# Who reads the quads' bank, and when: reordering VectorE's queue in a four-layer attention kernel

## The reference, cut to what matters

```python
q = nx @ Wq (+ bq);  k = kv @ Wk (+ bk);  v = kv @ Wv (+ bv)     # nx: layer norm of x, scaled and shifted
a = softmax(q @ k.T / sqrt(8) (masked), axis=-1)                  # per head
x = x + (gate *) ((a @ v) @ Wo (+ bo))
```

## Time and profile before

| | us |
|---|---|
| median of 3 runs | 1131.72 (1129.71 to 1132.47) |
| the profiled execution | 1134.09 |
| its span, first to last instruction | 1131.5 |
| stages (span): `l0` | 60 to 224 |
| `l0c` | 224 to 355 |
| perceptron and layer 1 | 355 to 655 |
| `l2`, `l3s`, `l3c` | 655 to 790, to 933, to 1063 |

### The profile page before, as it was taken

One profiled execution on the slowest core, in us unless ns is written; L12 is line 12 of the kernel. 1 busy time (PEld: TensorE's weight loads), 2 busy tenths in 40 slices (PEclk: granted clock), 3 DMA queues, 4 the chain that ended last, 5 costly groups with the idle time before them and its releaser, 6 DMA issues.

```text
span 1131.5 us, 28818 instructions
## 1 busy us (share of the span) xinstructions
PE 1045.1 (92%) x11743; PEld 651.6 (58%) x11743; DVE 803.4 (71%) x1971; ACT 572.0 (51%) x801; POOL 673.9 (60%) x776
## 2 busy tenths in 40 slices
PE   6899999999988999999999699998999999998998
PEld 4445555565555775666666445555555566555476
DVE  6788888788873534676677878878888777787321
ACT  1034434566566455444444156665555656665553
POOL 6578887777864341121114588887877656587430
PEclk8699999999999999999999699999999999999799
DMA  4300000000000102000000000000000000000001
GB/s 176 132 8 3 20 12 12 21 19 13 20 21 20 39 28 88 7 6 6 6 6 18 7 13 2 2 2 2 2 1 2 2 2 2 2 2 2 1 28 47
DMA packets 9283, 22.76 MB, mean 20 GB/s; under 512 B 1393, under 2 KB 1649, under 8 KB 8769
## 3 DMA queue, kind: packets, MB, share of 16 engines
q1 hardware_dynamic: 9152, 20.94, 5.5%
HBM read 18.77 MB, written 2.15 MB: 18 GB/s over the span
## 4 chain that ended last, share of the span: by engine, by line
PE 69%; DVE 17%; issue 5%; POOL 5%; ACT 4%; DMA 0%; DVEq 0%; POOLq 0%; ACTq 0%
PE weighed L653 11%; PE scores L626 8%; PE row_scores L595 7%; DVE negmax L1159 6%; PE scores L837 6%; PE weighed L676 5%; PE quads L534 3%; PE row_scores L837 3%; PE quads L545 2%; PE weighed L848 2%; DVE bn L1037 2%; PE scores L638 2%; PE quads L559 2%; PE scores L552 2%; ACT p L1588 2%
## 5 line engine op out<-in xcount | busy, mean ns | idle before, releaser
L1159 DVE TENSOR_REDUCE negmax<-row_scores 128x8 f32<-128x616 f32 (+1 forms) x312 | 299.9, 961 | 80.4 <-PE row_scores L595 62.6
L1588 ACT ACTIVATE p<-scores 128x1024 f32<-128x1024 f32 (+1 forms) x256 | 247.7, 1018 | 197.6 <-PE scores L638 197.6
L626 PE MATMUL scores<-qblk,work 32*77 32x512 f32 (+1 forms) x1280 | 206.0, 625 | 13.1 <-ACT p L1588 4.9
L1756 POOL TENSOR_TENSOR kblk_r<-work,pack_const 128x308 fp32r<-128x308 f32 (+1 forms) x160 | 133.9, 838 | 90.3 <-PE row_scores L595 71.3
L653 PE MATMUL weighed<-p,v 77*32 77x128 f32 (+1 forms) x5120 | 175.5, 278 | 2.5 <-DVE nat L1184 2.5
L595 PE MATMUL row_scores<-kblk_r,qr 32*128 32x308 f32 (+1 forms) x624 | 142.3, 447 | 27.5 <-DVE negmax L1159 27.2
L1746 POOL TENSOR_TENSOR qblk<-work,pack_const 128x512 f32<-128x512 f32 x160 | 166.3, 1039 | 0.2
L653 PEld LDWEIGHTS weighed<-p,v 77*32 77x32 f32 (+1 forms) x5120 | 131.8, 110 | 41.2 <-issue 38.5
L595 PEld LDWEIGHTS row_scores<-kblk_r,qr 32*128 32x128 f32 x624 | 62.0, 187 | 129.6 <-issue 94.4
L1184 DVE STREAM_TRANSPOSE nat<-weighed 128x256 f32<-128x256 f32 x160 | 71.1, 445 | 39.9 <-PE weighed L653 34.1
L1793 POOL TENSOR_TENSOR attn<-nat,rden 128x128 f32<-128x128 f32 x160 | 65.7, 410 | 48.0 <-DVE rden L1189 47.5
(11 more groups left out here) (295 smaller groups left out, 1878.3 us busy)
## 6 DMA issues: line engine op xcount, KB each, us to landing
shared<-gates_hbm SPq DMA_DIRECT2D x24, 256.0 KB, 3.3
shared<-in_ctx_tok SPq DMA_DIRECT2D x15, 154.0 KB
pack_w_l<-in_w_l SPq DMA_DIRECT2D x1, 2058.5 KB, 11.2
x<-in_x_tok SPq DMA_DIRECT2D x8, 256.0 KB, 6.6
out_x<-x SPq DMA_DIRECT2D x8, 256.0 KB, 2.0
layers_w<-in_w_l SPq DMA_DIRECT2D x1, 1289.0 KB, 9.6
ctxT<-in_ctxT SPq DMA_DIRECT2D x1, 1232.0 KB, 9.3
layers_w<-in_w_ada SPq DMA_DIRECT2D x1, 582.0 KB, 5.0
```

The lines of the kernel that those rows point to most:

```text
L626: mm = e.matmul(scores[0:nk, g, :], k_of[q % 3][at, s * nk:(s + 1) * nk], qblk[n % 2][at, :], start=layer.mask != "qk", stop=False, skip_g ...
L1159: e.tensor_reduce(negmax[q % 2][:, 2 * h:2 * h + 2, s * NJ:(s + 1) * NJ], row_banks(n, h)[:, :, 0:NJ * nk].rearrange("p g (j k) -> p g j k ...
L1588: e.activation(p[n % 2][0:nk, 8 * h:8 * h + 8, :], scores[0:nk, 2 * h:2 * h + 2, :].rearrange("p g (j q) -> p (g j) q", j=NJ), ACT.Exp, bi ...
L1756: e.tensor_tensor(kblk_r[n % 2][:, 0:NJ * nk].rearrange("p (j k) -> p j k", j=NJ), k_of[q % 3][:, s * nk:(s + 1) * nk].unsqueeze(1).to_bro ...
```

## The change

1. VectorE in narrow layers (77 keys): `scale_normed` (own norms) and `residual` are deferred to the next slot, behind `row_max(t + 5, 1)`. `spread_max` moves from cl 2 to cl 3 outside of `l0`, ahead of `turn_blocks`; PE's `turn_max` moves with it, behind `weigh`.
2. PE in `l3s`: `quad_work`, with the values in it, comes ahead of `weigh`, as in `l0`.
3. ScalarE takes the queries of `l0c` (the zeroing of dead sequences goes into the norm's scale and shift by two small products in the setup) and the raw x of `l3c`. The residual of `l3s` is copied from PSUM by ScalarE (`take_out`) and added by GpSimd (`add_out`), with a semaphore `x_summed`.
4. In `l2` one of three norm statistics of cl 2 moves to cl 1.

```diff
-        at = [last - 2, last, last, last]
+        at = [last - 2, last - 1, last, last] if it.kind == "l2" else [last - 2, last, last, last]
...
         def q_by_act(q):
-            return q >= 2 * NB + 3
+            return NB <= q < 2 * NB or q >= 2 * NB + 3
...
# PE
-                    if cl == 3 and qi + 1 in quads:
-                        w.wait_ge(nblk_done, qi + 2)
                     if masked:
                         mask_rows(t + 6, 0, False)
+                        if cl == 3 and qi + 1 in quads:
+                            w.wait_ge(nblk_done, qi + 2)
+                    if is_wide(t):
                         quad_work(t, qi, cl)
                         if t - 1 in jobs:
                             weigh(t - 1)
...
-                        if cl == 2 and qi + 1 in quads:
+                        if cl == 3 and qi + 1 in quads:
                             turn_max(qi + 1)
                         quad_work(t, qi, cl)
-                    if masked and cl == 2 and qi + 1 in quads:
+                    if is_wide(t) and cl == (2 if masked else 3) and qi + 1 in quads:
                         turn_max(qi + 1)
...
# VectorE, setup
+                w.wait_ge(dve_setup, DVE_AT["live_bc"])
+                for t in (l0A[1][:, :], l0mod[:, 3, :]):
+                    e.tensor_tensor(t, t, live_bc[:, :], ALU.mult).then_inc(dve_setup, 1)
...
# VectorE, attention
+                def deferred(t):
+                    return t in jobs and t + 1 in jobs and layer_of(t // QUAD).nk != S
+                def own_affine(t):
+                    if t in norm_at and not norm_at[t].family:
+                        scale_normed(norm_at[t])
+                def own_residual(t):
+                    qi, cl = divmod(t, QUAD)
+                    if cl == 2 and qi - 2 in quads and not sum_by_pool(qi - 2):
+                        residual(qi - 2)
...
                     if t + 5 in jobs:
                         row_max(t + 5, 1)
+                    if deferred(t - 1):
+                        own_affine(t - 1)
+                        own_residual(t - 1)
...
+                    if not masked and cl == 3 and qi + 1 in quads:
+                        spread_max(qi + 1)
                     if t in norm_at and norm_at[t].family:
                         scale_normed(norm_at[t])
-                    if wide and cl == 2 and qi - 2 in quads:
-                        residual(qi - 2)
-                    if cl == 2 and qi + 1 in quads:
+                    if wide:
+                        own_residual(t)
+                    if masked and cl == 2 and qi + 1 in quads:
                         w.wait_ge(negmax_turned, qi + 2)
                     if t - 1 in jobs:
                         turn_blocks(t - 1)
-                    if cl == 2 and qi + 1 in quads:
+                    if masked and cl == 2 and qi + 1 in quads:
                         spread_max(qi + 1)
-                    if t in norm_at and not norm_at[t].family:
-                        scale_normed(norm_at[t])
+                    if not deferred(t):
+                        own_affine(t)
                     if not masked:
                         stats(t)
-                    if cl == 1 and qi + 3 in quads and layer_of(qi + 3).name == "l3c":
-                        take_x(qi + 3)
-                    if cl == 2 and qi - 2 in quads and not wide:
-                        residual(qi - 2)
+                    if not wide and not deferred(t):
+                        own_residual(t)
...
# ScalarE
+            def take_x(q): ...   # e.copy(xn[q % 3], quad_bank), the same waits as VectorE's had
+            def take_out(q):
+                w.wait_ge(wo_done, q + 1)
+                w.wait_ge(x_summed, q - 3 * NB - 1)
+                e.copy(gated[q % 2][:, :], out_bank(q)).then_inc(wo_read, 1)
...
+                    if cl == 2 and qi - 2 in quads and sum_by_pool(qi - 2):
+                        take_out(qi - 2)
+                    if cl == 1 and qi + 3 in quads and layer_of(qi + 3).name == "l3c":
+                        take_x(qi + 3)
...
# GpSimd
+            def add_out(q):
+                w.wait_ge(wo_read, q + 1)
+                w.wait_ge(x_biased, q - 2 * NB + 1)
+                xs = quad(x, q % NB)
+                e.tensor_tensor(xs, xs, gated[q % 2][:, :], ALU.add).then_inc(x_summed, 1)
...
+                    if cl == 3 and qi - 2 in quads and sum_by_pool(qi - 2):
+                        add_out(qi - 2)
```

More of the change, by code:

```diff
@@ L160 @@
              "dead4", "lift_rows", "neg_qk", "mk", "live_b", "dead_b", "lift_b", "neg_bk", "neg_bk_bf", "live_diag",
-             "l0mod1", "l0A1", "l0A2", "select", "ones_bf", "lift_cols", "neg_kq", "gates", "neg_kb", "live_bc"]
+             "l0mod1", "l0A1", "l0A2", "select", "ones_bf", "lift_cols", "neg_kq", "gates", "neg_kb", "live_bc", "l0A1_live", "l0mod_live"]
 DVE_AT = {name: k + 1 for k, name in enumerate(DVE_SETUP)}
@@ L289, in build @@
         attnT_done, wo_done, wo_read = sem("attnT_done"), sem("wo_done"), sem("wo_read")
-        x_gated, x_biased, ffn_biased = sem("x_gated"), sem("x_biased"), sem("ffn_biased")
+        x_gated, x_summed, x_biased, ffn_biased = sem("x_gated"), sem("x_summed"), sem("x_biased"), sem("ffn_biased")
         mlp_in, mlp_act, mlp_out, mlp_read, mlp_delta, mlp_added = (
@@ L317, in affine @@
                 i = ("l0", "l0c", "l0m").index(it.kind)
-                return l0A[i][:, seqs], l0mod[:, 3 * i, seqs], dve_setup, DVE_AT[f"l0A{i}"]
+                return l0A[i][:, seqs], l0mod[:, 3 * i, seqs], dve_setup, DVE_AT["l0mod_live" if i == 1 else f"l0A{i}"]
             if it.kind in ("l2k", "l2"):
@@ L351, in x_after, with sum_by_pool @@
         def x_after(q):
-            return (x_gated if layer_of(q).gated else wo_read), q + 1
+            return (x_summed, q - 3 * NB + 1) if sum_by_pool(q) else ((x_gated if layer_of(q).gated else wo_read), q + 1)
+        def sum_by_pool(q):
+            return layer_of(q).name == "l3s"
         def x_before(q):
@@ L1118, in scale_normed @@
                                 scale.unsqueeze(2).to_broadcast([128, QUAD, it.n]), ALU.mult).then_inc(ln_scaled, 1)
[L1120 to L1125, removed]
             def rotate(q, which):
@@ L1140, in take_q @@
             def take_q(q):
-                layer, c = layer_of(q), q % NB
+                layer = layer_of(q)
                 w.wait_ge(proj_q, q + 1)
@@ L1144, in take_q @@
                 w.wait_ge(qr_done, q - 2)
[L1145 to L1150, removed]
-                    bias = W[layer.name + "_qb"]
-                    e.tensor_scalar(q_of[q % 3], quad_bank[:, :], bias, None, ALU.add).then_inc(q_done, 1)
+                e.tensor_scalar(q_of[q % 3], quad_bank[:, :], W[layer.name + "_qb"], None, ALU.add).then_inc(q_done, 1)
             def row_max(n, h):
@@ L1567, in take_q, with take_x @@
                 w.wait_ge(qr_done, q - 2)
-                e.activation(q_of[q % 3], quad_bank[:, :], ACT.Identity, bias=W[layer_of(q).name + "_qb"]).then_inc(q_done, 1)
+                if layer_of(q).gated:
+                    done = e.copy(q_of[q % 3], quad_bank[:, :])
+                else:
+                    done = e.activation(q_of[q % 3], quad_bank[:, :], ACT.Identity, bias=W[layer_of(q).name + "_qb"])
+                done.then_inc(q_done, 1)
+            def take_x(q):
+                w.wait_ge(raw_turned, q % NB + 1)
+                w.wait_ge(proj_q, q - 2)
+                w.wait_ge(proj_k, q - 2)
+                w.wait_ge(proj_v, q - 2)
+                e.copy(xn[q % 3], quad_bank[:, :]).then_inc(raw_done, 1)
+            def take_out(q):
+                w.wait_ge(wo_done, q + 1)
+                w.wait_ge(x_summed, q - 3 * NB - 1)
+                e.copy(gated[q % 2][:, :], out_bank(q)).then_inc(wo_read, 1)
             def take_v(q):
```

## The result

The changed kernel takes 1120.37 us (median of 4 runs, 1117.01 to 1120.94), the kernel before 1131.47 (4 runs beside it, 1129.71 to 1132.47). The ratio is 0.9897, 95% interval 0.9874 to 0.9921: faster by 11.1 us, 1.0%. The forecast was 1123.3 (1114 to 1130). The profiled execution took 1120.89, with a span of 1119.1.

A forecast was written before the change was run, and what follows sets the result against it. No engine was full; time was lost in handshakes, chiefly PE waiting for VectorE's maximum. Terms -5.9 (l2), -3.0 (l0c), -1.9 (l3c), +2.0 (l3s), +0.4 (start) sum to -8.4 us: 1123.3 from a 1131.72 median, range 1114 to 1130.

The forecast's parts named there:

- l2: 5.9 forecast: In l2, of the 9.5 us that PE waits for VectorE's maximum (`negmax`), 3.6 stay and 5.9 go.
- The 0.15 kept for the moved statistic: In l2's cl 1, 0.15 us of PE's 0.56 us wait stays, because one statistic moves there from cl 2.
- l0c: 3.0 forecast: In l0c, 3.3 us of PE's waits go, less 0.3 for the family norm, whose `hat` now follows the spreading: 3.0.
- l3c: 1.9 forecast: In l3c, 2.4 us of waits go, less 0.5 for the last quads, where GpSimd's `qblk` ends the wait: 1.9.
- l3s: +2.0 forecast: In l3s, the new order's gains and losses by slot: +3.4 us in four quads, two even, -1.4 in the last two.
- The term for the values: In l3s, values projected before the weighing let scores start without waiting for ScalarE's copy; 0.74 us was lost in each quad.
- Rival B: In l3s the new order costs nothing, so 5.9 us is gained instead of 2.0 lost: 1115.4 us, chance 0.2.
- rival D: In l3s weighing, transposing, maximum and half 0 set every slot's period: 14.4 us lost, not 2.0; 1135.7 us, chance 0.1.
- The residual of l3s at nothing: In l3s, moving the residual to ScalarE and GpSimd costs 0: covered by the weighing in cl 2, GpSimd waits anyway.
- Rival C: In narrow quads the stall moves on (longer split, GpSimd late with `qblk`), losing half of 10.8 us: 1128.7 us, chance 0.17.
- Rival E: The edits do nothing visible because ScalarE, with two exponentials in short slots, ends the loop: 1131 to 1133 us, chance 0.03.
- Start: +0.4 forecast: At the start, the first spreading comes one slot later, right before the first shift: at most 0.65 us, taken as +0.4.

## Why the prediction was right, point by point

**l2: 5.9 forecast, 6.4 measured.** The step holds. The wait for `negmax` was to fall to 3.6 and is 2.9. In quads 17 to 19 no wait is listed any more in front of the row scores in cl 2 and 3; it isn't under 0.2 everywhere, since 0.21 is left in quad 20 and 0.34 where the maxima are those of 128 keys. Undoing the deferral brings back 5.2, undoing the spreading 3.0. What the prediction didn't see is why the spreading has to move: not only to clear the way to the maximum, but because the deferred `hat` would delay the split that the turning product waits for (1.4 us in l2 with only the spreading back in cl 2, 1.6 with the deferral alone, none after). The 0.15 kept for the moved statistic was a cost of nothing.

**l0c: 3.0 forecast, 4.9 measured.** The mechanism was right and a term was mis-sized: the take was costed at nothing because ScalarE has room, which is true but the wrong side of the ledger. The query of 0.69 us also left VectorE's queue ahead of a maximum. Put back, it costs 1.6. Without it my number stands: 3.0 forecast for the deferral and the spreading, 3.3 measured for the two.

**l3c: 1.9 forecast, 2.7 measured** (2.4 in its first five quads). Here the number was near for the wrong reason, and that is luck. I gave the whole 1.9 to the deferral and the spreading and nothing to raw x. With raw x back on VectorE the five quads are only 0.6 shorter than before, and PE waits 2.3 us for `negmax`, about the 2.4 of before; raw x off VectorE's queue is worth 1.8 of the 2.4. With it off, the deferral adds 0.2.

In both stages I had read the gain off the listed waits, 3.3 and 2.4 us, as an upper bound, and it isn't one: l0c gained 4.9 where 3.3 were listed. Short waits between matmuls are not in the list: PE's idle time in that window fell by 3.6 (7.13 to 3.49), and its busy time by another 1.2 for the same 1623 matmuls, which fits a PE that counts as busy while it waits among overlapping matmuls; no view here shows that directly.

**l3s: +2.0 forecast, +1.4 measured**, twice: in the change and alone on the kernel before (144.54). From one first half of row scores to the next, in a quad with statistics, the forecast was +0.45, 0, -0.1 and +0.5. Before, the starts 849.66 and 859.76 of the earlier trace rows and their neighbours give 3.98, 4.62, 5.48 and 4.20; after, the fence above and the next quad give 4.29, 4.63, 5.28 and 4.64: +0.31, 0.01, -0.20, +0.44. In cl 0 the maximum began at 839.29, where PE's wait of 0.66 shows that the delay is not hidden. By groups of quads (from exponential to exponential) the agreement is less good than in the sum: the first four quads lost 2.0 us where I had 3.4, the next two gained 0.2 where I had them even, and the last two gained 0.35 where I had 1.4. The first and the last group were both sized too large, and their errors cancel in part. The term for the values holds: the 0.74 between row scores and scores is gone in all eight quads. Rival B (the order costs nothing, 5.9 gained) and rival D (a ring in every slot, +14.4) are both refuted by the stage.

**The residual of l3s at nothing**: confirmed, 144.48 either way, with GpSimd's additions at a mean of 1.27 us.

**Rival C** (the stall moves on in the narrow stages): not seen; l2 gained more than forecast. The casts of the split, on which it rested, last after the change as in the earlier trace rows:

```profile
L1161 DVE CAST max_parts<-negmax x40: 130/150/874, 48.5 to 1024.8; 128x64 bf16<-128x64 f32 x40
```

But the longest, 0.87 us, is the first of them in both kernels, at 46.8 and 48.5 us in the setup, and so says nothing of a narrow quad. The eight casts of l2 lasted 0.15 to 0.78 before (0.31 in the median) and 0.13 to 0.76 after (0.23). So what lengthens them in l2 is about as present as it was, and after the change no wait for the split is listed there. The rule of the Trainium skill that was weighed there (SBUF — State Buffer, Who interferes with whom) is neither confirmed nor refuted by this: it speaks of how long an instruction is blocked, not of who waits for it.

**Rival E** (ScalarE ends the loop): not seen, and its ground was misread. Two exponentials take 2.0 us (1.02 each), while the shortest slots of l2 are 3.3.

**Start: +0.4 forecast, +1.9 measured.** Of that, 1.4 stands in the trace ahead of anything that the change touches: PE's second projection (L549) starts at 18.17 instead of 16.72. In other traced runs with the same code there it starts between 16.7 and 19.6, so this is no effect of the change. The 0.4 that remain agree with the forecast, but are too little beside that to count as shown. The spreading stands right in front of the first shift, as forecast: it starts at 60.75, and the shift at 61.49.

**Middle: 0 forecast, -1.9 measured.** At 278.51 us behind the stretch's first exponential the same matmul starts in both traces, and the 1.9 arise in the 21 us behind that. The granted clock was lower there before (0.80 and 0.60 in the two windows from 620 to 660) than after (0.83 and 0.74), which makes some 24 us at the lower level against 17, an estimate from these windows. In the other traced runs the middle takes 313.0 to 315.8 us. So the agreement of the sums (-8.4 and -12.4, or 1123.3 and 1120.4) is better told by stages: the attention layers from l0c on gave 12.6 where I had 8.8, while start, `l0`, middle and rest (+1.9, +0.3, -1.9, -0.1) cancel to 0.2. Of the 3.8 that the layers gave beyond the forecast, the takes, put at nothing, are the larger part (3.4 us where they were put back).

## What to carry over

Where two engines take turns over one buffer, look at the position of its reader in the reader's queue: here three reads of 0.65 to 0.69 us in a quad, moved from ahead of the maximum to behind it or to another slot, were worth most of 6.4 us in l2. Put everything that nobody waits for right behind such a reader, and ask of each moved piece both what it clears and what it now delays. Cost a piece that changes engines on both queues: it can be free where it goes and still be a gain where it leaves. When an edit of an order meets several slots, price it slot by slot; here one slot of four carried the whole gain (values first, with the spreading moved: -2.5 us) and the others only cost (+4.4).

## What the runs showed of the hardware

The attention stages repeat to 0.1 to 0.3 us from run to run, but the whole does not: runs of one kernel differ by 4 to 7 us and more (1112.86 to 1120.06 with l3s' old order). What differs between the traces, beside the start, is how long TensorE is granted its lower level, 1.2 GHz instead of 2.4, in two places. Ahead of l2, the kernel before (first row) and after (second):

```profile
640.00:660.00 20.00, 15.40 (x103) 8.48 (x103) 12.87 (x33) 5.72 (x11) 15.36 (x17) 0.60 0.03 8
```

```profile
640.00:660.00 20.00, 16.94 (x147) 9.33 (x146) 13.80 (x43) 8.60 (x15) 14.18 (x16) 0.74 0.03 9
```

And behind l3c, the kernel after (first two rows) and the one with the residual on VectorE, whose code there is the same:

```profile
1020.00:1040.00 20.00, 17.10 (x217) 8.97 (x221) 10.19 (x35) 9.15 (x13) 14.38 (x17) 0.81 0.00 1
1040.00:1060.00 20.00, 18.53 (x184) 10.74 (x179) 7.30 (x28) 10.80 (x14) 7.26 (x10) 0.76 0.01 2
```

```profile
1020.00:1040.00 20.00, 15.63 (x253) 8.94 (x257) 10.88 (x37) 10.64 (x13) 15.67 (x19) 1.00 0.01 2
1040.00:1060.00 20.00, 17.19 (x175) 10.67 (x168) 6.88 (x24) 13.57 (x19) 9.93 (x11) 1.00 0.00 1
```

With the clock at 1.00 in these 40 us the end of the kernel (from quad 39's first exponential) takes 79.3 us, with the dips 83.6. From 600 to 620 PE was busy for 19.9 us before and 19.5 after, at a granted clock of 1.00; from 620 to 640, just ahead of the first pair of rows, it was busy for only 13.5 and 11.3, and the clock was 0.80 and 0.83. So the level fell in a stretch in which PE stood idle for a third of the time before and over 40% of it after. What decides between one run and the next was not tried. For the reader of such runs it means that a difference of 2 us between two kernels can be read from a stage whose clock is 1.00, and not from a median.
